# Running-maximum products of an attention block: k's high part alone, two matmuls side by side on half arrays, four to a visit

## The reference

```python
y = x * rsqrt(mean(x * x) + RMS_EPS) * rms_w          # after a layer norm
q, k, v = split(einsum('bsm,cm->bsc', y, w_in))       # 32, 8 and 8 heads of 64
q, k = rope(q), rope(k)
qk = einsum('bghsd,bgxpd->bghsp', q, k) * 64 ** -0.5
attn = softmax(where(causal, qk, -inf))
y = einsum('bghsd,...->bsm', attn @ v, w_out)
```

## Time and profile before

| | |
|---|---|
| median of three runs | 1968.36 us |
| profiled execution | 1969.3 us, its span 1967.5 us (1.8 us lie outside the span) |
| PE busy | 1915.5 us (97%) |
| POOL busy | 1423.1 us (72%) |
| DVE busy | 1233.3 us (63%) |
| ACT busy | 937.3 us (48%) |
| pieces (L572) | 1280 matmuls, 348 ns mean as recorded |
| low parts (L816) | 1280 instructions, 919 ns mean |

### The profile page before, as it was taken

The page is one execution under the profiler, slowest core; times in us unless marked ns, Lnnn a source line. Parts: engine busy times, 40 slices in busy tenths (PEclk is TensorE's granted clock), DMA queues, the critical chain, the costliest instruction groups (busy, mean ns, idle before and its releaser), DMA issues. The chain is left out here.

```text
span 1967.5 us, 55165 instructions
## 1 busy us (share of the span) xinstructions
PE 1915.5 (97%) x21382; PEld 1182.7 (60%) x21382; DVE 1233.3 (63%) x3283; ACT 937.3 (48%) x1997; POOL 1423.1 (72%) x1627
## 2 busy tenths in 40 slices
PE   4999999999999999999999999999999999999999
PEld 3566666666666666666666666666654444444444
DVE  7787588668768866876886688577736563122221
ACT  4465556556565565665565556556732212120110
POOL 1799999999999999999999999999950002131221
PEclk6999999999999999999999999999999999999999
DMA  6342252254215224422522332244146520000000
GB/s 212 68 80 40 47 101 55 48 85 74 60 33 120 50 50 76 80 50 46 106 50 45 65 68 47 45 83 106 37 147 220 213 86 1 22 0 21 5 16 22
DMA packets 301812, 136.79 MB, mean 70 GB/s; under 512 B 248576, under 2 KB 285696, under 8 KB 300032
## 3 DMA queue, kind: packets, MB, share of 16 engines
q1 hardware_dynamic: 301568, 133.43, 30.3%
HBM read 49.48 MB, written 25.17 MB: 38 GB/s over the span
## 5 line engine op out<-in xcount | busy, mean ns | idle before, releaser
L816 POOL TENSOR_TENSOR pl<-p 128x512 f16<-128x512 f32 (+3 forms) x1280 | 1137.7, 919 | 38.7 <-ACT p L655 35.6
L655 ACT ACTIVATE p<-a_ps 128x512 f32<-128x512 f32 (+3 forms) x1280 | 677.4, 532 | 552.9 <-PE a_ps L588 331.1
L731 DVE TENSOR_REDUCE mpart<-a_ps 128x1 f32<-128x512 f32 x768 | 508.5, 685 | 130.9 <-PE a_ps L572 126.4
L604 PE MATMUL a_ps<-v,p 128*128 128x65 f16 x4352 | 527.7, 193 | 6.1 <-POOL pl L816 5.6
L606 PE MATMUL a_ps<-v,p 128*128 128x64 f16 x4352 | 530.2, 194 | 0.0
L608 PE MATMUL a_ps<-v,pl 128*128 128x65 f16 x4352 | 527.0, 192 | 0.0
L604 PEld LDWEIGHTS a_ps<-v,p 128*128 128x128 bf16 x4352 | 412.5, 97 | 109.5 <-issue 7.6
L606 PEld LDWEIGHTS a_ps<-v,p 128*128 128x128 bf16 x4352 | 405.9, 97 | 108.1
L588 PE MATMUL a_ps<-q_lm,k_h 128*128 128x512 f16 (+3 forms) x1280 | 444.4, 347 | 0.0
L587 PE MATMUL a_ps<-q_hh,k_hl 128*128 128x512 f16 (+3 forms) x1280 | 443.5, 347 | 0.0
L572 PE MATMUL a_ps<-k_hl,q_hh 128*128 128x512 f16 (+3 forms) x1280 | 428.8, 348 | 8.6 <-issue 4.6
(11 more groups left out here) (101 smaller groups left out, 2278.0 us busy)
## 6 DMA issues: line engine op xcount, KB each, us to landing
yh<-attn_scratch SPq DMA_DIRECT2D x32, 512.0 KB, 4.5
raw<-ffn_t SPq DMA_DIRECT2D x12, 1024.0 KB, 5.1
attn_scratch<-o_turn SPq DMA_DIRECT2D x32, 256.0 KB, 3.0
attn_scratch<-o_turn_late SPq DMA_DIRECT2D x32, 256.0 KB, 3.1
wraw<-w_in_t SPq DMA_DIRECT2D x8, 768.0 KB, 5.1
resid_scratch<-raw SPq DMA_DIRECT2D x4, 1024.0 KB, 4.4
raw<-w_out_t SPq DMA_DIRECT2D x16, 256.0 KB, 3.7
x<-resid_scratch SPq DMA_DIRECT2D x4, 1024.0 KB, 8.2
```

Of the source, the lines that this page charges most:

```text
L604: nc.tensor.matmul(o, weights, v[:, par, j, 0:VU], start=(j == 0 and t == 0), stop=False, skip_group_check=True)
L655: nc.scalar.activation(p32[:, i % RING, r * P:CHUNK], sbank(i)[:, r * P:CHUNK], ACT.Exp, scale=SCALE).then_inc(exp_done, 1)
L731: nc.vector.reduce_max(mpart[:, u % 2, t, kk:kk + 1], bank, AX.X).then_inc(maxs_used, 1)
L816: nc.gpsimd.tensor_tensor(pl[:, i % RING, cols], p32[:, i % RING, cols], p_high[:, i % RING, cols], ALU.subtract).then_inc(low_ready, 1)
```

## The change

The maxima are taken from k's high part alone. A piece contracts over 64 rows instead of 128, and two pieces form a pair: one uses rows 0 to 63 of the array (q's high part there, against `k_h1`, which has k's high part in rows 0 to 63), the other rows 64 to 127 (q's high part again, against `k_hl`, which has it there). The two pieces of a pair are of neighbouring query tiles and the same keys (`query_and_key_tile`), and PE waits for both of their banks before the first. Four pieces, two pairs, follow each other directly in a "gang". `PIECE_STEPS` gives way to `GANG_STEPS`, which names the step of each of the 40 gangs of a group, and `JOB_STEPS` has other numbers. The number of pieces, of DVE reductions, of projections and of DMAs stays.

```diff
-JOB_STEPS = ((0, 2, (1, 9, 13, 17)), (0, 3, (30, 44, 50, 54)), (1, 0, (86, 90, 113, 120)), (1, 1, (139, 144, 148, 152)))
+GANG = 4
+JOB_STEPS = ((0, 2, (0, 4, 10, 16)), (0, 3, (26, 27, 42, 53)), (1, 0, (88, 101, 118, 123)), (1, 1, (141, 146, 151, 155)))
-PIECE_STEPS = {(0, 4): (5, 8), (0, 5): (11, 17), (0, 6): (18, 24), ...
+GANG_STEPS = {(0, 4): (6, 9), (0, 5): (12, 15), (0, 6): (18, 20), ... (1, 2): (155,), (1, 3): (159,)}
...
-    for (ahead, u), (begin, end) in PIECE_STEPS.items():
-        for i in range(KEY_TILES[u]):
-            pieces[begin + i * (end - begin) // KEY_TILES[u]].append((ahead, u, i))
+    for (ahead, u), steps in GANG_STEPS.items():
+        for gang, n in enumerate(steps):
+            pieces[n] += [(ahead, u, GANG * gang + i) for i in range(GANG)]
...
+def query_and_key_tile(u, i):
+
+    pair, second = divmod(i, 2)
+    both, kk = divmod(pair, u // HG + 1)
+    return 2 * both + second, kk
...
-                def max_piece(ahead, u, i):
+                def max_gang(ahead, u, i):
...
-                    bank = take_bank("piece", ahead, u, i)
-                    width = CHUNK if kk < c else (t + 1) * P
-                    nc.tensor.matmul(bank[:, 0:width], q_hh[:, c % 2, h, t * P:(t + 1) * P],
-                                     k_hl[:, par ^ ahead, kk * CHUNK:kk * CHUNK + width], start=True, stop=True)\
-                        .then_inc(maxs_ready, 1)
+                    for n in range(GANG):
+                        if n % 2 == 0:
+                            banks = [take_bank("piece", ahead, u, i + m) for m in (n, n + 1)]
+                        rows, keys = ((slice(0, DH), k_h1), (slice(DH, P), k_hl))[n % 2]
+                        t, kk = query_and_key_tile(u, i + n)
+                        width = CHUNK if kk < c else (t + 1) * P
+                        nc.tensor.matmul(banks[n % 2][:, 0:width], q_hh[rows, c % 2, h, t * P:(t + 1) * P],
+                                         keys[rows, par ^ ahead, kk * CHUNK:kk * CHUNK + width], start=True, stop=True)\
+                            .then_inc(maxs_ready, 1)
...
-                    for piece in pieces[:1]:
-                        max_piece(*piece)
+                    for piece in pieces[:GANG:GANG]:
+                        max_gang(*piece)
```

## The result

The changed kernel takes 1959.48 us (median of 4 runs, 1958.57 to 1961.57) where the kernel before, run beside it, takes 1969.95 (4 runs): a ratio of 0.995, 95% interval 0.9938 to 0.9962. So it is faster by 10 us. The forecast was 1939, 30 us less: the sign is right, and two thirds of the gain did not come. The profiled execution is 1961.57 us long, its span 1959.8 (1967.5 before).

What follows compares the result with a forecast made beforehand. PE was taken to set the pace at 174.2 us a group; shortened to 168.7, it leaves POOL's 170.5. 8 x (174.2 - 170.5) = 30 us off gives 1939 us, range for 8 in 10 1914 to 1987.

Steps and rivals of the forecast that it cites:

- Pairs overlap: On PE, a pair's two pieces run at the same time and cost the wider half, saving 13.5 us a group.
- a change of rows: On PE around each gang, switching between 128 and 64 rows: 0.10 us each, 80 a group, 8 us a group.
- the rivals on both: On PE: pairs don't overlap, 2032 us, chance 0.06; row changes empty the array, 1985, 0.18, or balance the saving, 0.09.
- an upper bound: For a change of rows on PE: the engine empties and starts again, 0.195 us.
- POOL's pace is then 170.5 us, above PE's 168.7. So the group comes to 170.5: Whole group: POOL's 166.5 us of work plus 4 of waits exceeds PE's total, so POOL sets the group's time.
- Those for exponentials ... go when PE leads: POOL's waits for exponentials, 4.5 us a group, vanish because PE may run five steps ahead.
- Those at projections: POOL's waits for a projection's chain through DVE and ACT stay, kept at 4 us a group.
- POOL's queue of up to five steps hides a PE wait of that size: At steps 9, 15, 20: PE's waits behind DVE are covered by POOL's queue; 16 to 24 us in all without cover.
- a price of 2 to 3 us: PE's waits at three tight places, steps 9, 15, 20, up to 1 us each: a group's worst case.
- the rival with the banks: PE's waits for banks or keys are not covered: 1951 to 1963 us, say 1954, chance 0.08.
- DMAs are as many as before, so their instructions ... on SP add nothing: On SP, an unchanged number of DMAs was costed at nothing.
- my zero: At a group's start, key transposes standing later on SP cost nothing; bound 1.7 us at seven starts, 12 us.

Runs made afterwards that it cites:

- Experiments 5: Changed kernel with POOL's rotary addition narrowed to 8 of 64 columns of each head, part of the computation left out: 170.7 us a group.
- 9: Changed kernel without the weights' high part times v's low part in every second step, and one DVE instruction replaced by one on ACT: 169.9 us a group.
- 12: Changed kernel with PE shortened, one DVE instruction replaced on ACT and POOL's rotary additions narrowed, all at once: 1908.01 us, 164.9 us a group.
- experiment 3: Changed kernel with DVE's full reductions reading only 256 of 512 columns: 1965.5 to 1988.1 us over its runs, undisturbed groups 0.7 us shorter.
- 11: Changed kernel with last-group result loads after the last q_hh transpose, chunk 3 projections at steps 27, 35, 43, 55 and five gangs moved: 1945.53 us.
- experiment 2: Changed kernel with the last group's four result loads started after the last q_hh transpose of chunk 3 instead of before its first: 1952.22 us.
- experiment 6: Changed kernel without the product of the weights' high part with v's low part in every second step: 35 us slower than the changed kernel.

## Why the prediction was wrong

**Right: PE's side.** Pairs overlap (0.004 us), a change of rows costs 0.095 us where 0.10 was taken, and the rivals on both fall. (The 0.10 was half of an upper bound; that it came so near is luck.) Added up from start to start, less the waits, PE's work in the group from 415.60 is 167.7 us; 168.7 was forecast. POOL's busy time stayed at 166.2.

**The step that failed: "POOL's pace is then 170.5 us, above PE's 168.7. So the group comes to 170.5".** It takes the larger of two sums over a whole group. The group is the sum over stretches, and each has its own limit. In the first 35 us POOL, with narrow steps, waits for exponentials behind PE, which has two projections one step behind the other (L567) and gangs that wait for their banks; neither engine's total counts there, as the cut above shows. In the other 137 POOL is full and PE waits for it. POOL's idle in the first part was 3.1 us before, with two projections fewer up to step 28, and is 5.5 now; in the rest it was 4.5 and is 0.3. PE's waits, read from starts more than 0.11 us later than the columns before them allow, are 4.3 us in that group: 1.7 for banks, all within the first 38 us, 2.6 later, most of them for POOL or ACT. 167.7 + 4.3 = 172.0, and 166.2 + 5.8 = 172.0. Experiments 5, 9 and 12 show the balance in the rest. "Those for exponentials ... go when PE leads" is where it entered: PE does not lead in the first part, and 3.9 us a group stayed where none was forecast. Those at projections, kept at 4 from the earlier trace rows, were 3.4 in whole groups and fell to 1.8. In all 1.6 us a group are missing, 12 us in the first seven.

**"POOL's queue of up to five steps hides a PE wait of that size"** failed for the same reason. I had the place (steps 9, 15, 20) and a price of 2 to 3 us, and 1.7 came. But in those steps POOL had no queue to live on, as its idle there says. One place, a second pair that waits for a bank which a projection held:

```profile
428.19 0.39 PE L583 MATMUL a_ps<-k_h,q_hh 64*128 64x512 f16 x1
428.19 0.39 PE L583 MATMUL a_ps<-k_hl,q_hh 64*128 64x512 f16 x1
428.75 0.21 PE L583 MATMUL a_ps<-k_h,q_hh 64*128 64x128 f16 x1 [0.18 <-DVE v L771]
```

0.56 us between starts in place of 0.216. Which share of the 1.6 us the banks carry and which the two projections isn't settled: the undisturbed groups of experiment 3 give 0.7 us, and 11, which moved gangs with the projections, 0.9. The time fell into the range of the rival with the banks (1951 to 1963) and only in part for its reason, since no rival had the last group.

**"DMAs are as many as before, so their instructions ... on SP add nothing"** failed in one place. The count is the same, but the order against the gangs is not: the last group came to 166.0 us where 160.5 - 3.7 = 156.8 was forecast. That is 9 us, and experiment 2 gives back 8 of them. I had looked at SP's order at a group's start only. There my zero held: a wait for the keys stands as "issue" in the earlier trace rows, and behind 77.7 us no piece of the kernel after waits so. (Before, four groups' first pieces did, 3.2 us in all, where I wrote "once".)

In sum: 12 us from the first seven groups and 9 from the last are the 21 that the forecast lacks (the profiled span fell by 7.7, with 30 forecast).

## What to carry to other kernels

Where two engines stand within some per cent of each other, do not take the larger total: cut the group into stretches, take what is late in each, and add. A stretch may follow neither engine's work but the order and the buffers between them, as the first 35 us here. A saving on one of two level engines gives a fraction of itself until the other is cut too. And where a table moves work, look at every DMA in front of a gang, in the last group as well: its place counts, not its number.

## What the hardware showed unexpectedly

A DVE instruction with two inputs in SBUF can be held far longer than one POOL instruction: 9.14 and 8.78 us, 0.60 alone, while POOL ran eleven instructions back to back. By the Trainium skill ("SBUF — State Buffer", SBUF: two separate sides) such an instruction and a GpSimd one take a shared port pair as an exclusive lock, the later one blocked until the first is done. The traces agree that it is held up beside POOL, but here not for one instruction. In all ten cases (seven groups of experiment 6, three of 3) it ended 0.41 us behind the last of POOL's row. In the changed kernel, beside thirteen back to back, it took 1.50 us and ended 0.41 us behind the end of the second POOL instruction that it met, with the row still going on. So it got in at an end of a POOL instruction each time; why at the second there and only at the row's end here was not settled by these runs.
